# Expert slots of an attention and mixture-of-experts layer: the loop written out, one weight copy for each slot, the second bias through the gates, more buffers

## What is computed

```python
xf = x.reshape(b * t, d)
logits = xf @ Wg                                   # 16 experts
_, topi = jax.lax.top_k(logits, K)                 # K = 2
gates = jax.nn.softmax(jnp.where(mask, logits, -jnp.inf), axis=-1)
for e in range(E):
    h = jax.nn.silu(xf @ W1[e] + b1[e]) * (xf @ W11[e] + b11[e])   # 128 -> 256
    y = y + (h @ W2[e] + b2[e]) * gates[:, e, None]                # 256 -> 128
z = jax.nn.silu(xf @ Ws1 + bs1) * (xf @ Ws11 + bs11) @ Ws2 + bs2   # 128 -> 512 -> 128
return (y + z).reshape(b, t, d)
```

## Time and profile before

| | us |
|---|---|
| median of 3 runs | 773.39 |
| profiled execution, span | 773.9 |
| attention, to 571 us | 571.0 |
| norm, logits, slots, to 599.3 us | 28.3 |
| scatter beside the shared expert, to 644.1 us | 44.8 |
| 48 expert slots, to 749.7 us | 105.6 |
| gather, second norm, store, to 773.9 us | 24.2 |

### The profile page before, as it was taken

One profiled execution on the slowest core, in us unless ns is written; L12 is line 12 of the kernel. 1 busy time (PEld: TensorE's weight loads), 2 busy tenths in 40 slices (PEclk: granted clock), 3 DMA queues, 4 the chain that ended last, 5 costly groups with the idle time before them and its releaser, 6 DMA issues.

```text
span 773.9 us, 17695 instructions
## 1 busy us (share of the span) xinstructions
PE 688.3 (89%) x5442; PEld 523.0 (68%) x5443; DVE 534.2 (69%) x1874; ACT 419.2 (54%) x908; POOL 105.3 (14%) x172
## 2 busy tenths in 40 slices
PE   4799999979999997999999899999958987999940
PEld 3577777747777774777777577777744556878830
DVE  4687767678777777787767888776787523556536
ACT  4766555656655557655555766554533213454445
POOL 2000000000000000000000000000021773565540
PEclk9999999998999999899999999999976996999975
DMA  8300000040000004000000694000090112222224
GB/s 188 83 2 1 2 3 1 8 107 2 1 2 2 2 1 111 3 1 1 2 2 1 145 130 4 2 2 2 1 302 25 49 52 56 65 63 64 67 73 113
DMA packets 56260, 33.64 MB, mean 43 GB/s; under 512 B 23776, under 2 KB 49520, under 8 KB 56176
## 3 DMA queue, kind: packets, MB, share of 16 engines
q1 hardware_dynamic: 53616, 27.33, 17.6%
q0 software_dynamic: 2560, 5.26, 2.0%
HBM read 14.70 MB, written 9.48 MB: 31 GB/s over the span
## 4 chain that ended last, share of the span: by engine, by line
PE 61%; issue 12%; DVE 12%; POOL 6%; ACT 4%; DMA 3%; SPq 0%; POOLq 0%; DVEq 0%; ACTq 0%
PE ps_o L1079 16%; PE ps_t L961 16%; PE ps_s L1044 9%; PE ps_s L1050 8%; POOL x_sorted L480 4%; PE ps_o L1089 3%; PE ps_s L1193 3%; DVE q_hl L674 2%; PE ps_o L1208 2%; DMA y_rows<-y_sb,row_now 1%; DVE k_l L674 1%; ACT probsT L568 1%; PE ps_s L1048 1%; DVE probs L755 1%; POOL y_rows L490 1%
## 5 line engine op out<-in xcount | busy, mean ns | idle before, releaser
L755 DVE TENSOR_SCALAR_CACHE_REDUCE probs<-ps_s 128x512 f32<-128x512 f32 (+3 forms) x320 | 192.1, 607 | 77.2 <-PE ps_s L1050 75.2
L557 ACT ACTIVATE probs<-probs,nmax 128x128 f32<-128x128 f32 (+15 forms) x128 | 154.0, 1203 | 133.5 <-DVE nmax L762 133.1
L961 PE MATMUL ps_t<-ident,probs 128*128 128x128 f32 x1104 | 181.6, 281 | 17.5 <-ACT probs L529 11.1
L961 PEld LDWEIGHTS ps_t<-ident,probs 128*128 128x128 f32 x1104 | 130.8, 142 | 64.7 <-issue 23.5
L1079 PE MATMUL ps_o<-probsT,v_sb 128*64 128x128 f32 x2176 | 154.4, 280 | 0.0
L1044 PE MATMUL ps_s<-k_h,q_hl 128*128 128x512 f32 (+3 forms) x320 | 145.2, 454 | 6.1 <-issue 5.4
L1079 PEld LDWEIGHTS ps_o<-probsT,v_sb 128*64 128x64 f32 x2176 | 115.7, 137 | 38.6 <-issue 36.1
L1050 PE MATMUL ps_s<-k_l,q_hl 128*128 128x512 f32 (+3 forms) x320 | 128.5, 402 | 0.0
L568 ACT ACTIVATE probsT<-ps_t 128x512 f32<-128x512 f32 (+3 forms) x160 | 89.6, 560 | 62.2 <-PE ps_t L961 60.8
L771 DVE COPY probsT<-ps_t 128x512 f32<-128x512 f32 (+3 forms) x160 | 91.1, 570 | 25.7 <-PE ps_t L961 25.3
L1044 PEld LDWEIGHTS ps_s<-k_h,q_hl 128*128 128x128 f32 x320 | 62.4, 195 | 19.3 <-issue 14.8
(11 more groups left out here) (150 smaller groups left out, 790.3 us busy)
## 6 DMA issues: line engine op xcount, KB each, us to landing
k_h<-k_h SPq DMA_DIRECT2D x32, 128.0 KB, 2.3
k_l<-k_l SPq DMA_DIRECT2D x32, 128.0 KB, 2.4
w_up<-in_L_ffn_W SPq DMA_DIRECT2D x2, 2048.0 KB, 12.1
xg<-x_sorted SPq DMA_DIRECT2D x48, 64.5 KB, 1.8
x_sorted<-zeros SPq DMA_DIRECT2D x12, 256.0 KB, 9.5
act_s<-y_rows SPq DMA_DIRECT2D x8, 256.0 KB, 4.9
x_acc<-in_L_attn_tokens SPq DMA_DIRECT2D x4, 256.0 KB, 3.6
out<-x_acc SPq DMA_DIRECT2D x4, 256.0 KB, 2.3
```

The costliest lines, as they stand in the source:

```text
L557: nc.scalar.activation(probs[s % 2][h][:, 0:w], probs[s % 2][h][:, 0:w], ACT.Exp, bias=nmax[:, row], scale=SCALE, accum_out=rsum[:, row]). ...
L755: nc.vector.tensor_scalar(probs[s % 2][h][:, c * BANK:c * BANK + w], ps_s[n % RING][:, 0:w], 1.0, None, ALU.mult, ALU.max, accum_out=cmax[ ...
L961: return nc.tensor.transpose(dst, src, ident[:, :])
```

## The change

Slots. The loop is gone: 48 slots are written out on each engine, so that every wait is on a constant and every address but one is a constant. All that a slot needs of its expert lies side by side in `w_all` (512 up columns, 4 bias columns, 256 down columns, 772 in all) and is copied by one DVE instruction into `w_now`, with 3 buffers. `xg` has 6 buffers and `y_sb` has 4. The order within a slot is: up products of n, turn of n + 2, down products of n - 1. On POOL the copy of the row numbers is made straight from `xg` into a column of `row_all`, four slots ahead, and the DMA reads that column; DVE no longer copies row numbers, and POOL no longer has the wait for the landing of the DMA of two slots ago (ACT still waits for `y_out`, now of four slots ago).

Second bias. It is taken out of the slots. `gated` (each token's gate at its two experts) is made on DVE, turned on PE, copied by ACT, and multiplied with `b2_pad` (zero but for 16 rows in each of 8 blocks) at the end of each tile of `shared_down`. For that the gates are worked out before the shared expert and not after the slots.

Around it. `b2_pad` is set to zero by POOL at the start and loaded by eight DMAs of SP's queue; the three bfloat16 parts of `b2` are gone. The bias columns are loaded after the expert weights. `it` and `past` have 768 elements in place of 1664.

```diff
-            def send(n, b):
-                pool.wait_ge(row_noted, n + 1)
-                nc.gpsimd.tensor_copy(row_now[:, b:b + 1], row_all[:, bass.ds(n, 1)]).then_inc(row_set, 1)
-                pool.wait_ge(row_set, n + 1)
-                pool.wait_ge(y_ready, n + 1)
-                pool.sem_inc(sent, 1)
...
-            with pool.Fori(1, SLOT_TILES // 2) as i:
-                for b in range(2):
-
-                    pool.wait_ge(y_out[b], i * 16)
-                    send(i * 2 + b, b)
+            def note_row(n):
+
+                pool.wait_ge(xg_in[n % XB], 16 * (n // XB + 1))
+                nc.gpsimd.tensor_copy(row_all[:, n:n + 1], xg[:, n % XB, D:D + 1].bitcast(u32)).then_inc(row_noted, 1)
+
+            for n in range(4):
+                note_row(n)
+            for n in range(SLOT_TILES):
+                if n + 4 < SLOT_TILES:
+                    note_row(n + 4)
                 pool.wait_ge(row_noted, n + 1)
...
                 pool.wait_ge(y_ready, n + 1)
...
+                    out=y_rows, out_offset=bass.IndirectOffsetOnAxis(ap=row_all[:, n:n + 1], axis=0),
+                    in_=y_sb[:, n % YB, :], in_offset=None).then_inc(y_out[n % YB], 16)
```

```diff
+            act.wait_ge(gexp, 1)
+            nc.scalar.activation(gat[:, 1, :], gat[:, 0, :], ACT.Exp).then_inc(gexp, 1)
             for n in range(NC * SB):
...
+            x_turned(0)
+            x_turned(1)
+            for n in range(SLOT_TILES):
+                b = n % 2
+                act.wait_ge(w_ready, n + 1)
+                act.wait_ge(up_e, n * 2 + 1)
+                for m in range(HB):
+                    cols = slice(m * P, (m + 1) * P)
+                    nc.scalar.activation(sil[:, b, cols], ps_s[2 * b][:, cols], ACT.Silu,
+                                         bias=w_now[:, n % WB, UP + m:UP + m + 1]).then_inc(sil_e, 1)
+                if n + 2 < SLOT_TILES:
+                    x_turned(n + 2)
+                if n >= 1:
+                    y_out_of_psum(n - 1)
```

```diff
+            dve.wait_ge(gexp, 2)
+            link(nc.vector.tensor_scalar(gat[:, 2, :], gat[:, 1, :], 1.0, None, ALU.add))
+            link(nc.vector.reciprocal(gat[:, 2, :], gat[:, 2, :]))
+            link(nc.vector.tensor_tensor(gat[:, 3, :], gat[:, 1, :], gat[:, 2, :], ALU.mult))
+            for k in range(TOPK):
+                ins = nc.vector.tensor_tensor(gated[:, k], hot[:, k], gat[:, 2 + k, :].unsqueeze(2).to_broadcast([P, NT, E]),
+                                              ALU.mult)
+            link(ins)
+            nc.vector.tensor_tensor(gated[:, 0], gated[:, 0], gated[:, 1], ALU.add).then_inc(gated_ready, 1)
...
+            def weights_of(n):
+                if n >= WB:
+
+                    dve.wait_ge(down_e, n - WB + 1)
+                e = experts[n // IDS % 2][n % IDS]
+                nc.vector.tensor_copy(w_now[:, n % WB, :], w_all[:, bass.ds(e, 1), :]
+                                      .rearrange("p a n -> p (a n)")).then_inc(w_ready, 1)
```

```diff
                     for m in range(SB):
...
+                                         start=(m == 0), stop=False)
+                    mm = nc.tensor.matmul(ps_t[i % 2][:, j * P:(j + 1) * P], gatedT[:, t // GT8, :],
+                                          b2_pad[:, t % GT8, :], start=False, stop=True)
...
-                    nc.tensor.matmul(y, ones3[:, :], b2_rows[:, bass.ds(e * D, D)], start=True, stop=False)
...
+            for n in range(SLOT_TILES):
+                b = n % 2
+                pe.wait_ge(xgT_ready, n + 1)
+                pe.wait_ge(w_ready, n + 1)
+                for a in range(2):
                     for m in range(HB):
...
+                        mm = nc.tensor.matmul(ps_s[2 * b + a][:, m * P:(m + 1) * P],
+                                              w_now[:, n % WB, a * H + m * P:a * H + (m + 1) * P], xgT[:, b, :],
+                                              start=True, stop=True)
+                    mm.then_inc(up_e, 1)
+                if n + 2 < SLOT_TILES:
+                    turn_in(n + 2)
+                if n >= 1:
+                    expert_down(n - 1)
+            expert_down(SLOT_TILES - 1)
```

More of the change, by code:

```diff
@@ L611, in _ @@
                                      bias=bs_col[:, 0, m:m + 1]).then_inc(sil_done, 1)
-            def expert_slot(r, j, up=True, next=True, down=True):
-                n, b, o = r * ROUND + j, j % 2, 1 - j % 2
-                if next:
-                    act.wait_ge(xgT_psum, n + 2)
-                    nc.scalar.activation(xgT[:, o, :], ps_t[o][:, 0:P], ACT.Copy).then_inc(xgT_ready, 1)
-                if up:
-                    act.wait_ge(up_e, n * 2 + 1)
-                    for m in range(HB):
-                        cols = slice(m * P, (m + 1) * P)
-                        nc.scalar.activation(sil[:, b, cols], ps_s[2 * b][:, cols], ACT.Silu,
-                                             bias=w_now[:, b, UP + m:UP + m + 1]).then_inc(sil_e, 1)
-                if down:
-                    if not isinstance(n, int) or n >= 3:
-                        act.wait_ge(y_out[o], by_dma(n - 3, o, 2))
-                    act.wait_ge(down_e, n)
-                    nc.scalar.activation(y_sb[:, o, :], ps_o[o][:, 0:D], ACT.Copy).then_inc(y_ready, 1)
@@ new lines, in y_out_of_psum @@
+            def y_out_of_psum(n):
+                if n >= YB:
+                    act.wait_ge(y_out[n % YB], 16 * (n // YB))
+                act.wait_ge(down_e, n + 1)
+                nc.scalar.activation(y_sb[:, n % YB, :], ps_o[n % 2][:, 0:D], ACT.Copy).then_inc(y_ready, 1)
+            x_turned(0)
[4 more added lines that the diff above has]
+                act.wait_ge(up_e, n * 2 + 1)
+                for m in range(HB):
+                    cols = slice(m * P, (m + 1) * P)
[5 more added lines that the diff above has]
+                    y_out_of_psum(n - 1)
@@ L1155, in _ @@
                 shared_up(n)
+                if n == SB + 1:
+                    pe.wait_ge(gated_ready, 1)
+                    for k in range(NT // GT8):
+                        mm = turn(ps_o[0][:, k * P:(k + 1) * P],
+                                  gated[:, 0, k * GT8:(k + 1) * GT8, :].rearrange("p n e -> p (n e)"))
+                    mm.then_inc(gT_psum, 1)
+                if n == 2 * SB - 1:
+                    pe.wait_ge(gT_ready, 1)
+                    pe.wait_ge(b2_in, 16 * GT8)
                 if n % SB == SB - 1 and n >= SB:
@@ L1213, in _, with turn_in, expert_down @@
-            expert_slots(pe, expert_slot)
+            def turn_in(n):
+                pe.wait_ge(xg_in[n % XB], 16 * (n // XB + 1))
+                turn(ps_t[n % 2][:, 0:P], xg[:, n % XB, 0:D]).then_inc(xgT_psum, 1)
+            def expert_down(n):
+                pe.wait_ge(hid_e, n + 1)
+                if n >= 2:
+                    pe.wait_ge(y_ready, n - 1)
+                for m in range(HB):
+                    at = UPB + m * D
+                    mm = nc.tensor.matmul(ps_o[n % 2][:, 0:D], hid[:, n % 2, m * P:(m + 1) * P],
+                                          w_now[:, n % WB, at:at + D], start=(m == 0), stop=(m == HB - 1))
+                mm.then_inc(down_e, 1)
```

249 lines of the change are left out of this document (85 added, 164 removed).

## The result

| | before | changed |
|---|---|---|
| median, us | 773.88 (773.01 to 776.36) | 750.11 (747.10 to 752.41) |
| profiled execution: span | 773.9 | 747.4 |
| first issue of `xg` (SP's queue) | 642.24 | 643.84 |
| first turn of rows on PE | 644.10 | 645.78 |
| first `y_sb` | 650.34 | 650.64 |

The ratio is 0.9689, with a 95% interval from 0.9662 to 0.9717: 3.1% faster. The forecast was 751.8 in a range of 743 to 765.

What follows compares the result with a forecast made beforehand. POOL's chain was taken to bound the slots at 2.04 us each. Landing 643.2, first `y_sb` 6.3, 47 steps 75.2, copy and DMA start 0.28 and 0.79, landing 2.3, rest 24.2 sum to 752.3, less 0.5: 751.8 us, range 743 to 765.

Steps and rivals of the forecast that it cites:

- landing of the first rows: First `xg` load before the slots: 644.1 less 0.9, so landed at 643.2 us.
- to the first `y_sb`: From first landing to first `y_sb`: 6.3 us as before, assuming the clock falls again; about 3.8 at the high level.
- The central step: In the slots POOL's chain sets the 2.04 us pace; freed, POOL needs 1.47 and the pace becomes 1.6.
- The choice between 1.46 and 1.66: PE's slot without the bias product: 1.66 us, or 1.46 if that product also costs the unexplained 0.20.
- the 0.20 that no row explained: On PE in a slot, the bias product's load comes 0.20 us later than the pace of the other loads.
- The cause of 0.82: POOL's idle 0.82 us between its cast and indirect DMA, expected to become 0.30 without the wait for its own cast.
- the rivals: On POOL's gap: 0.82 us belongs to the indirect DMA, not the wait; POOL stays the limit, 770 us, chance 0.11.
- Less than 0.30 I exclude: POOL's gap between cast and indirect DMA: not under 0.30 us, because 31 gaps of the scatter are that long.
- The long copy: DVE's `w_now` copy in each slot grows from 512 to 772 columns and takes 0.73 us at most.
- the slower rival: In each slot the long copy holds POOL, 0.73 on top of the 0.82 gap: 2.72 us, 805 us total, chance 0.04.
- Ahead of the slots: Four terms before the first `xg` load: smaller `it` -1.1, smaller compare -1.0, ACT tables +0.7, DVE gates +0.5; sum -0.9 us.
- Writing the loop out removes jumps from engines that waited anyway: The slots' loop written out on each engine: listed among the edits expected to give nothing.

## Why the prediction was right, and where it wasn't

By the profiled span, the sum was 752.3 and the measured one 747.4. Term by term:

| term | predicted | measured |
|---|---|---|
| landing of the first rows | 643.2 | 645.8 |
| to the first `y_sb` | 6.3 | 4.9 |
| 47 slots | 75.2 (1.6 each) | 69.5 (1.48) |
| copy and start of the DMA | 1.1 | 1.1 |
| landing, and the rest | 26.5 | 26.2 |

- **The central step held: POOL's chain was the limit, and without it PE's is.** The 47 steps took 96.0 us before and take 69.5 now, so the pace gave 26.5 us. That the span is shorter by 26.5 as well is because 2.7 lost in the attention were made good by 1.0 ahead of the slots, 1.4 up to the first `y_sb` and 0.3 at the end.
- **The pace was set 0.12 too high.** The choice between 1.46 and 1.66 went the wrong way: the 0.20 that no row explained was the bias product's, as the run with the product put back shows. With the rows at hand the fair value was the lower one, since a gap beside the only instruction of another kind is most simply that instruction's. The rest of the 1.48 is the 0.35 lost once in eight slots, which the prediction had not seen: DVE's load of eight expert numbers.
- **The cause of 0.82 was not found.** The part on POOL takes out three things, the wait for its own cast, the landing wait and the raise, and doesn't say which had made the gap; the rivals call it "the wait". With the wait for its own copy alone it is 0.28, and the raise brings the 0.82 back. The sum was right because the change removes all three. With wait and raise kept the kernel comes out at 779.
- **"Less than 0.30 I exclude" was wrong.** The gap is 0.16 behind a copy. The 0.30 in the earlier trace rows is that of two DMAs in a row, not a minimum for a DMA.
- **The long copy.** Predicted at most 0.73, measured 0.56 where nothing meets it and up to 0.82 where a DMA of POOL's does. It stretches the DMA from 0.98 to 1.09 in most slots and at most to 1.195 in this kernel, and to 1.358 at most in the run with the raise, where the slower rival needed 0.73 on top in each slot. What a meeting costs depends on when the copy starts, which the prediction didn't ask. The copy beside the DMA at 663.73 in the changed kernel, and the one beside the DMA at 663.50 in the run that waits for POOL's own copy:

```profile
664.14 0.56 DVE L884 COPY w_now<-w_all 128x772 f32 x1
```

```profile
663.72 0.56 DVE L881 COPY w_now<-w_all 128x772 f32 x1
```

  The first starts 0.41 behind the DMA's start, and the DMA ends 0.12 behind the copy's end, 0.11 late. The second starts 0.22 behind it, and neither takes longer. The slots of ten traces fall into the same four cases. A copy that runs when the DMA starts lets it end 0.84 to 0.86 behind the copy's end, if that is later than the DMA's own 0.98 (the compare of the earlier trace rows as well: 609.61 and 610.45). One that starts 0 to 0.28 behind the DMA's start costs nothing. One that starts 0.3 to 0.5 behind it lets the DMA end 0.11 to 0.13 behind the copy. One that starts later, up to 0.75, is itself held, and of 772 columns ends 0.36 behind the DMA. By the rule of the Trainium skill, SBUF — State Buffer, "SBUF: two separate sides", the one of the two that starts first holds the shared port pair for its whole instruction and the other stands still. The traces agree that each can hold the other up and disagree on the whole instruction, as the second copy shows, and the measurement decides.
- **Ahead of the slots the sum was right and its terms weren't.** From the end of the attention to the landing it is 72.33 before and 71.32 now, -1.0 against -0.9. But the smaller `it` (0.99 us now) didn't shorten DVE's step of four elements beside it, 2.73 before and 2.80 now:

```profile
577.88 2.80 DVE L691 TENSOR_SCALAR rstd<-mv 128x4 f32<-128x4 f32 x1
...
593.17 1.28 ACT L566 ACT_TABLE_LOAD   x1 [6.25 <-DVE gat L795]
594.70 1.28 ACT L572 ACT_TABLE_LOAD   x1
...
596.79 0.75 DVE L802 SCALAR_TENSOR_TENSOR act_s<-ps_s,bs_col,sil_s 128x512 f32<-128x512 f32 x1 [1.10 <-ACT sil_s L572]
```

  What replaced it: the rows behind that step are shorter (1.12 for four, 1.90 in the kernel before), and DVE is done with them 9.6 us behind the attention's last product in place of 10.2. That this is due to the smaller `it` was not tested. The two table loads cost 0.85 (0.7 predicted), the gates beside the first DMAs nothing (0.5 predicted), and the smaller compare gave 1.3 (1.0 predicted).
- **Not foreseen: 2.7 us lost in the attention**, whose last product moves from 571.77 to 574.46. "Writing the loop out removes jumps from engines that waited anyway" looked only at the loop that was written out, not at the one that stayed, and no term of the sum stood for it. The better pace hid this in the total.
- **The clock fell, as assumed, but for less long.** Granted clock (third number from the right) while the first slots run, against the earlier trace rows:

```profile
646.00:648.00 2.00, 1.84 (x9) 1.74 (x9) 0.00 (x0) 0.79 (x3) 0.74 (x4) 0.52 0.57 141
648.00:650.00 2.00, 2.00 (x14) 2.00 (x14) 1.08 (x3) 0.98 (x5) 0.00 (x0) 0.63 0.26 64
```

  PE had idled 2.8 us instead of 9.5 before the first turn; the low level (1.2 GHz) then lasted until about 649.5, and the first `y_sb` came 4.9 us behind the first turn, between the 3.8 and the 6.3 of the prediction.
- **Span and time were mixed.** The prediction took the span of 773.9 for the profiled execution's time and called it 0.5 over the median. In the profiled execution of every kernel whose time is known, the time is 1.7 to 2.0 above the span (749.17 for 747.4), so that execution was some 2 us over its median, while the changed kernel's was 0.9 under it. By the spans the sum was 4.9 too high, by the medians 751.8 on 750.11 is 1.7 too high. The 3.2 us between the two are mostly where the two profiled executions happened to lie, and so luck.

## What to carry to other kernels

When one engine's chain draws the others out, look for the slot in which it isn't yet the limit: its length is what the next engine will give, and a gap there beside the only instruction of an unusual kind is first of all to be put down to that instruction, as it proved here. Test each instruction of a waiting protocol by itself, as the one of 0.04 us can be the one that costs 0.54 in every slot. And look at the loops that stay: a loop of three passes, with two jumps back on each engine, cost 13.5 us here, more than half of what the whole change gave.

## What the runs showed of the hardware

- A semaphore raised by POOL between its waits and an indirect DMA: gap 0.82 us behind POOL's copy; with the waits on the DMA itself and a copy of POOL's just before: 0.28; with that copy's wait long satisfied: 0.16. Behind the end of a late `y_sb` of ACT's the DMA starts after 0.75.
- VectorE's copy within SBUF and POOL's indirect DMA hold each other up only at some offsets: with the copy's start 0 to 0.28 us behind the DMA's, none; 0.3 to 0.5 behind it, the DMA ends 0.11 to 0.13 behind the copy; with the copy already running, 0.84 to 0.86 behind it.
- At a jump back of the attention's loop: 2.6 to 3.1 us without work on TensorE; on VectorE 3.3 to 3.8, which is its wait for TensorE, or 5.4 to 6.1 in the kernels with the slots written out on all engines. The attention's last product stood at 574.46 with the loops, at 570.12 with VectorE's written out, and at 561.00 with all of them written out: 13.5 us for a loop of three passes.
- The bias product (three rows of bfloat16, its address in a register): 0.17 us idle before its load and 0.16 to the next load, in each slot.
- VectorE's load of eight registers: 0.65 us in which nothing else of it runs; one register in each slot left no trace in the pace.
